# Expert stage of a small language model: first and third products on the two row halves of the array, experts summed on VectorE

## The chip, the cores and the metric

The kernel runs on one core of one Trainium2 chip. The metric is the device time of one execution in microseconds (us). Before the change it is 245.43 us, the median of 3 runs (244.35 to 245.56).

A core has four engines that compute: TensorE (PE in the profile; PEld is its loading of weights), VectorE (DVE), ScalarE (ACT) and GpSimd (POOL). Each works through a program of its own, in order. They wait for each other through semaphores. TensorE writes its results into PSUM, eight banks of 2 KB in each of 128 partitions; the other engines read them there.

## What is computed

The reference is a tower for 8 rows of 256 tokens with 64 channels: a convolution net on embedded tokens, an attention without softmax, and then a transformer block, whose mixture of experts is what the change touches. In float32:

```python
flat = _rmsnorm(x, ln2_w).reshape(-1, Cx)          # 2048 tokens, 64 channels
probs = jax.nn.softmax(flat @ router_w.T, axis=-1)
tp, ti = jax.lax.top_k(probs, TOPK)                # 2 of 8 experts
tp = tp / (jnp.sum(tp, axis=-1, keepdims=True) + 1e-09)
weights = jnp.sum(tp[..., None] * jax.nn.one_hot(ti, NE, dtype=flat.dtype), axis=1)
out = jnp.zeros_like(flat)
for e in range(NE):
    hh = jax.nn.silu(flat @ w1[e].T) * (flat @ w3[e].T)     # 170 hidden channels
    out = out + weights[:, e:e + 1] * (hh @ w2[e].T)
return x + out.reshape(Bx, Tx, Cx)
```

All experts are computed for all tokens; the gate weights, zero for six of eight, choose.

## The kernel before

**Tiling.** The 2048 tokens are 16 tiles of 128, in four groups of four tiles, called pairs in the code (a pair of batch rows, `PAIRS`). The 8 x 170 hidden channels are laid out in `CH` = 11 blocks of up to 128: eight with the first 128 channels of an expert each, three with the remaining 42 channels of up to three experts. A *unit* u (0 to 43) is one pair with one block: 128 hidden channels by 512 tokens, one PSUM bank. Pair n is u // 11, the place in it i = u % 11; `ORDER` (line 18) gives the block.

**Precision.** A float32 value is kept as two float16 numbers, high and low. `fTs` (line 159) holds the transposed normalised input of a tile: the high parts of the 64 channels in partitions 0 to 63, the low parts in 64 to 127. The weights `w1h` and `w3h` (lines 149, 150) lie twice in the partitions, and their index w says high or low. So one matmul over 128 partitions gives (high + low) times the high weight, a second one (high + low) times the low weight.

**One unit** (TensorE's loop is at lines 1909 to 1963) goes through the engines like this:

1. TensorE: two matmuls of 512 columns with `w1h` into a bank of `A_BANK` (0 and 4 in turn), two with `w3h` into a bank of `B_BANK` (3 and 5 in turn).
2. ScalarE, line 814: silu of the first product into `sil`, two buffers in turn.
3. VectorE, line 1330: the third product times `sil`, into `hh`, a ring of six. It is called hh u in the prediction.
4. ScalarE, line 799 (`high_part`): cast of hh u to float16, the high part.
5. GpSimd, line 414 (`low_part`): hh u minus the high part, the low part.
6. TensorE, `down` (line 1844): when the blocks of two experts are there (`FILLED`), their second product for one tile, in three parts (high by high, high by low, low by high), 9 or 12 matmuls of 128 or 64 columns. A bank of `DOWN_BANK` (6 and 1 in turn) holds two experts of four tiles.

ScalarE's loop (line 801) issues silu u and then the cast of u-1. Silu u waits for hh u-2 (line 813). TensorE's first product of u waits for silu u-2, its third product for hh u-2 (lines 1914 to 1921).

**Mixing.** `mix` (line 1254) multiplies a bank of second products with the gate weights into `moe` in SBUF; `mix_add` (line 1261) multiplies the next one in PSUM and adds it to that. So VectorE leaves two partial sums of 512 columns per pair, and TensorE adds them, and the two experts in each, by multiplying with the float32 identity `identf` into bank 2 (`sum_up`, line 1895). `result` (line 1270) adds the residual. The last pair ends in another way (`last_rows_in`, `last_even`, `last_result`, and `last_high` and `last_low` on TensorE), which the change leaves nearly alone.

**Input of a pair.** GpSimd's `third_root` and `third_split` (line 384) make the high and low parts of the normalised rows in `shl`; `f_transposed` on TensorE (line 1720) transposes them into PSUM; `f_rows` on ScalarE (line 741; pairs 0, 2 and 3) or `router_rows` on VectorE (line 1173; pair 1) copies them to `fTs`; `routed` on TensorE (line 1736) gives the router's products, `router_in`, `ranks`, `ranks_end` and `gates` on VectorE the gate weights, with an exponential on ScalarE between (line 746). For pairs 0 and 1 this happens in the attention ahead of the expert stage, beside the batch rows b = 6 and 7 of its loop. For pairs 2 and 3 it is put between units: GpSimd's root after low part 4 and 13, its split after low part 7 and 16 (lines 501 and following), VectorE's rows at u = 7 and 16, the transposes at u = 10 and 20, ScalarE's copy ahead of silu 11 and 21.

The order of all this is written out by hand, in one loop for each engine:

```python
# ScalarE, line 801
for u in range(PAIRS * CH):
    ...
    act.wait_ge(S["a_ps"], u + 1)
    if u >= 2:
        act.wait_ge(S["hh_ready"], u - 1)
    nc.scalar.activation(sil[:, u % 2, :], bank[A_BANK[u % 2]][:, :], ACT.Silu, ...)
    if u:
        high_part(u - 1)
```

## Time and profile before

| | |
|---|---|
| median of 3 runs | 245.43 us (244.35 to 245.56) |
| the profiled execution, its own time | 245.12 us |
| its span in the trace | 243.3 us |
| granted TensorE clock, mean | 0.997 of full speed |
| TensorE matmuls busy | 206.2 us (85% of the span) |
| VectorE busy | 178.8 us (73%) |
| ScalarE busy | 153.6 us (63%) |
| GpSimd busy | 144.1 us (59%) |

The span runs from the first to the last instruction of the trace; 1.8 us of the execution's time lie around it. A matmul's record runs from its start to the end of its result, so two records that follow each other overlap: the step from start to start says how long it holds the array. The same holds for ScalarE and VectorE, whose next instruction can begin some 0.1 us ahead of the end of the last.

### The profile page before, as it was taken

The numbers are of one execution on the slowest core, as the hardware profiler recorded it, in microseconds if no ns is written. First come the engines' busy times: TensorE is split into PE (matmuls) and PEld (weight loads), VectorE is DVE, ScalarE is ACT, GpSimd is POOL, SyncE is SP. The second block draws the span as 40 slices with busy tenths as digits, with TensorE's granted clock in tenths as the row PEclk, the third lists the DMA queues.
The fourth block names the chain that finished last, engine by engine and source line by source line (L and its number), as shares of the span: only waits on it lengthen the run. The fifth ranks groups of instructions, "written<-read, shape, count | busy, mean of one in ns | idle before, by whom it ended". The sixth has DMA issues, their size and how long they took to land.

```text
span 243.3 us, 7308 instructions
## 1 busy us (share of the span) xinstructions
PE 206.2 (85%) x2828; PEld 134.7 (55%) x2836; DVE 178.8 (73%) x417; ACT 153.6 (63%) x277; POOL 144.1 (59%) x196
## 2 busy tenths in 40 slices
PE   7987788888897997976888979988899899888991
PEld 3654446445554755655666757644465465465671
DVE  4224665959878599979975879569868964999586
ACT  2368867277794677876356556577675579576670
POOL 6840000133677657574568896737989784777771
PEclk9999999999999999999999999999999999999998
DMA  2577300000000000000000000000000000010010
GB/s 43 118 164 176 83 5 3 0 3 3 3 1 3 3 3 3 3 3 0 3 3 0 3 0 3 4 0 1 3 3 1 3 23 3 0 24 0 3 24 22
DMA packets 8396, 4.51 MB, mean 19 GB/s; under 512 B 7556, under 2 KB 7852, under 8 KB 8364
## 3 DMA queue, kind: packets, MB, share of 16 engines
q1 hardware_dynamic: 8364, 4.06, 7.3%
q8 instruction: 23, 0.38, 0.6%
q14 instruction: 9, 0.07, 0.1%
HBM read 3.53 MB, written 0.52 MB: 17 GB/s over the span
## 4 chain that ended last, share of the span: by engine, by line
PE 41%; DVE 29%; ACT 12%; issue 10%; POOL 6%; DVEq 0%; POOLq 0%; ACTq 0%
PE bank L1369 39%; DVE shared L1330 3%; DVE nmx L1120 2%; ACT early L671 2%; ACT oTx L662 1%; ACT oT L656 1%; DVE shared L968 1%; DVE L L1297 1%; POOL shared L414 1%; DVE oT L1150 1%; ACT qT L814 1%; DVE early L861 1%; ACT early L565 1%; DVE nmr L1129 1%; DVE s L1167 1%
## 5 line engine op out<-in xcount | busy, mean ns | idle before, releaser
L1369 PE MATMUL bank<-early 64*64 64x256 f32 (+5 forms) x556 | 56.5, 352 | 10.8 <-DVE early L861 2.7
L414 POOL TENSOR_TENSOR shared<-shared 128x512 f16<-128x512 f32 x44 | 51.3, 1166 | 17.1 <-ACT shared L799 14.4
L1369 PEld LDWEIGHTS bank<-early 64*64 64x64 f32 (+3 forms) x556 | 30.7, 126 | 28.4 <-issue 5.2
L1330 DVE SCALAR_TENSOR_TENSOR shared<-bank,qT 128x512 f32<-128x512 f32 x44 | 29.7, 687 | 12.4 <-ACT qT L814 11.5
L799 ACT CAST shared<-shared 128x512 f16<-128x512 f32 x44 | 27.0, 614 | 12.1 <-DVE shared L1330 12.1
L814 ACT ACTIVATE qT<-bank 128x512 f32<-128x512 f32 x44 | 26.3, 597 | 10.5 <-PE bank L1369 10.3
L349 POOL TENSOR_TENSOR stat<-stat,neghalf 128x4 f32<-128x4 f32 x8 | 8.2, 1021 | 37.0 <-DVE stat L946 35.7
L1369 PE MATMUL bank<-onehot,w3h 128*128 128x512 f16 x88 | 26.3, 380 | 3.7 <-DVE shared L1330 3.5
L1369 PE MATMUL bank<-onehot,w1h 128*128 128x512 f16 x88 | 26.2, 379 | 0.3 <-ACT qT L814 0.3
L481 POOL TENSOR_TENSOR oTx<-oT,oTx 128x512 f16<-128x512 f32 x16 | 18.5, 1159 | 13.0 <-ACT oTx L662 12.9
L1369 PE MATMUL bank<-w2xh,shared 128*128 128x128 f16 (+1 forms) x240 | 22.4, 209 | 2.8 <-POOL shared L414 2.4
L1369 PE MATMUL bank<-qT,shared 64*64 64x128 f32 (+1 forms) x320 | 19.0, 326 | 5.5 <-DVE shared L968 2.9
L1369 PE MATMUL bank<-w2h,shared 128*128 128x64 f16 x384 | 22.7, 193 | 0.0
L1369 PEld LDWEIGHTS bank<-w2xh,shared 128*128 128x128 f16 x240 | 15.7, 98 | 10.2 <-POOL shared L414 4.6
L1120 DVE TENSOR_REDUCE nmx<-bank 128x2 f32<-128x512 f32 (+1 forms) x24 | 16.0, 687 | 7.2 <-PE bank L1369 6.9
L732 ACT ACTIVATE qT<-bank 128x512 f32<-128x512 f32 x24 | 14.3, 598 | 8.3 <-PE bank L1369 8.2
L861 DVE TENSOR_TENSOR early<-early 128x512 f32<-128x512 f32 x10 | 6.9, 692 | 17.0 <-ACT early L565 16.5
L1369 PEld LDWEIGHTS bank<-w2h,shared 128*128 128x128 f16 x384 | 18.3, 98 | 0.0
L1369 PEld LDWEIGHTS bank<-qT,shared 64*64 64x64 f32 x320 | 11.1, 132 | 12.8 <-issue 6.8
L656 ACT ACTIVATE oT<-bank 128x512 f32<-128x512 f32 x16 | 9.6, 597 | 12.8 <-PE bank L1369 12.7
L1369 PEld LDWEIGHTS bank<-onehot,w3h 128*128 128x128 f16 x88 | 7.8, 98 | 16.3 <-DVE shared L1330 8.4
L968 DVE TENSOR_TENSOR shared<-bank,trimul 128x512 f32<-128x512 f32 x16 | 11.0, 688 | 6.2 <-PE bank L1369 6.1
(228 smaller groups left out, 460.2 us busy)
## 6 DMA issues: line engine op xcount, KB each, us to landing
early<-in_tcn_w_dram SPq DMA_DIRECT2D x2, 320.0 KB, 4.2
w1s<-in_w1m_dram SPq DMA_DIRECT2D x2, 256.0 KB, 3.6
qT<-in_w3m_dram SPq DMA_DIRECT2D x2, 256.0 KB, 3.8
out_dram<-L SPq DMA_DIRECT2D x8, 64.0 KB, 1.7
qw<-in_attn_q_dram SPq DMA_DIRECT2D x4, 64.0 KB, 2.5
hTs<-in_w2m_dram SPq DMA_DIRECT2D x1, 256.0 KB
cos<-in_cos_t_dram SPq DMA_DIRECT2D x2, 96.0 KB, 2.5
sin<-in_sin_t_dram SPq DMA_DIRECT2D x2, 96.0 KB, 2.4
```

The lines of the kernel that those rows point to most:

```text
L349: nc.gpsimd.tensor_tensor(stat[:, dst, g4], stat[:, src, g4], neghalf[:, 0:4], ALU.pow) \
L414: nc.gpsimd.tensor_tensor(hhx[:, i, 1, :], hh[:, u % RING, :], hhx[:, i, 0, :], ALU.subtract).then_inc(S["lo_ready"], 1)
L481: nc.gpsimd.tensor_tensor(oTx[:, g % 2, 1, :, :], oT[:, g % 2, :, :], oTx[:, g % 2, 0, :, :], ALU.subtract).then_inc(S["o_low"], 1)
L656: nc.scalar.mul(oT[:, g % 2, :, :].rearrange("p a (cc t) -> p cc a t", cc=2), banks[:, 6:8, 0:256].rearrange("p cc (a t) -> p cc a t", a=4 ...
L732: nc.scalar.activation(pT[:, b % 2, u, :], bank[5 + (3 * b + u) % 2][:, :], ACT.Exp).then_inc(S["exp2_ready"], 1)
L799: nc.scalar.copy(hhx[:, i, 0, :], hh[:, u % RING, :]).then_inc(S["hi_ready"], 1)
L814: nc.scalar.activation(sil[:, u % 2, :], bank[A_BANK[u % 2]][:, :], ACT.Silu, scale=1.0 / FFN_SCALE).then_inc(S["sil_ready"], 1)
L861: V_.tensor_tensor(x_, x_, hid2[:, 2 * s:2 * s + 2, :], ALU.add).then_inc(S["x_ready"], 1)
L968: V_.tensor_tensor(om[:, g % 2, :].rearrange("p (x j t) -> p x j t", x=2, t=64), banks[:, 4:6, 0:256].rearrange("p x (j t) -> p x j t", t=64),
L1120: V_.tensor_reduce(nmx[:, g, h0:h0 + nh], bank[4 - (3 * b + u) % 2][:, :].rearrange("p (n s) -> p n s", n=nh), AX, ALU.max, negate=True).t ...
L1330: V_.scalar_tensor_tensor(hh[:, u % RING, :], bank[B_BANK[u % 2]][:, :], HH_SCALE / FFN_SCALE, sil[:, u % 2, :], ALU.mult, ALU.mult).then_ ...
L1369: return nc.tensor.matmul(out_, l_, r_, start=a, stop=z, skip_group_check=skip)
```

## The change

The normalised rows are laid out so that the high parts stand in both halves of the partitions, and in a second block the low parts in both: GpSimd's split writes the two middle parts of the new tile `shf`, a new copy on ScalarE (`f_twice`) writes the outer ones, eight transposes instead of four follow, and `f_rows` and `router_rows` copy 1024 columns instead of 512. The copy for pairs 0 and 1 stands after the exponentials of batch rows 5 and 6, that for pairs 2 and 3 ahead of silu 9 and 19.

A unit has six matmuls of 512 columns over 64 partitions each: the first product on partitions 0 to 63 and the third on 64 to 127, in turn, with the parts high by high, high by low and low by high. The product of the low parts is left out.

From u = 4 the third product has three banks in turn (7, 3, 5), and TensorE waits for hh u-3; `sil` has four buffers, and silu u waits for hh u-4. VectorE adds up the four parts of a pair in one partial sum (`first_mix` to `fourth_mix`) and adds the two experts of it in `result`; `sum_up` is gone. The downs and the mixings stand one to two units later than before. The gates' scratch moves from bank 7 to bank 2. The diff, cut to its core:

```diff
+        shf = shared[:, 9216:10240].bitcast(f16).rearrange("p (x a w c) -> p x a w c", x=2, a=4, w=4)
...
-        fTs = onehot[:, :, :].rearrange("p a b -> p (a b)").bitcast(f16).rearrange("p (g c) -> p g c", c=P)
+        fT2a = onehot[:, :, :].rearrange("p a b -> p (a b)").bitcast(f16).rearrange("p (a x t) -> p a x t", a=2, x=2)
+        fT2b = sTs[:, :, :].rearrange("p g t -> p (g t)").rearrange("p (a x t) -> p a x t", a=2, x=2)
+        fT2 = [fT2a[:, 0], fT2a[:, 1], fT2b[:, 0], fT2b[:, 1]]
...
-        sil = qT[:, :, 3, :]
-        moe = qst[:, :, :, :, :, :].rearrange("p a b c d e -> p (a b c d e)")[:, 0:4 * 2 * NE * C].bitcast(f32) \
-            .rearrange("p (k t e c) -> p k t e c", k=NE // 2, t=4, e=2)
+        sil = [qT[:, 0, 3, :], qT[:, 1, 3, :], qT[:, 0, 0, :], qT[:, 0, 1, :]]
+        moe = qst[:, :, :, :, :, :].rearrange("p a b c d e -> p (a b c d e)")[:, 0:2 * 4 * 2 * C].bitcast(f32) \
...
-        A_BANK, B_BANK, DOWN_BANK, SUM_BANK, LAST_BANK = (0, 4), (3, 5), (6, 1), 2, (0, 7)
-        geP = bank[7][:, 0:256].rearrange("p (a i j) -> p a i j", a=4, j=NE)
-        lP = bank[7][:, 256:288].rearrange("p (a e) -> p a e", a=4)
-        sumP, recP = bank[7][:, 288:292], bank[7][:, 292:296]
+        A_BANK, DOWN_BANK, ROW_BANK, LAST_BANK = (0, 4), (6, 1), 2, (0, 2)
+        geP = bank[2][:, 0:256].rearrange("p (a i j) -> p a i j", a=4, j=NE)
+        lP = bank[2][:, 320:352].rearrange("p (a e) -> p a e", a=4)
+        sumP, recP = bank[2][:, 352:356], bank[2][:, 356:360]
+
+        def third_bank(u):
+
+            return bank[(3, 5)[u % 2] if u < 4 else (7, 3, 5)[(u - 4) % 3]]
...
-                split(shl[:, p % 2, :, :, :], s2[:, p % 2, :, :], "fsplit_ready")
+                split(shf[:, p % 2, :, 1:3, :], s2[:, p % 2, :, :], "fsplit_ready")
...
+            def f_twice(p):
+                act.wait_ge(S["fsplit_ready"], p + 1)
+                nc.scalar.copy(shf[:, p % 2, :, 0:4:3, :], shf[:, p % 2, :, 1:3, :]) \
+                    .then_inc(S["f_twice"], 1)
+
             def f_rows(p, b_):
                 act.wait_ge(S["trf_ps"], p + 1)
-                nc.scalar.copy(fTs[:, 4 * p:4 * p + 4, :].rearrange("p a b -> p (a b)"),
-                               bank[b_][:, 0:256].bitcast(f16)).then_inc(S["fTs_ready"], 1)
+                nc.scalar.copy(fT2[p].rearrange("p x t -> p (x t)"), bank[b_][:, :].bitcast(f16)) \
...
+                if b >= 5:
+                    f_twice(b - 5)
...
+                if u == 9:
+                    f_twice(2)
+                if u == 19:
+                    f_twice(3)
...
-                if u >= 2:
-                    act.wait_ge(S["hh_ready"], u - 1)
-                nc.scalar.activation(sil[:, u % 2, :], bank[A_BANK[u % 2]][:, :], ACT.Silu,
+                if u >= 4:
+                    act.wait_ge(S["hh_ready"], u - 3)
+                nc.scalar.activation(sil[u % 4], bank[A_BANK[u % 2]][:, :], ACT.Silu,
...
+            def weigh(n_, k):
+
+                d_ = downs(DOWN_BANK[k % 2], slice(0, 4))
                 dve.wait_ge(S["w2_ps"], 16 * n_ + 4 * k + 4)
-                link(V_.tensor_tensor(downs(b_, tt), downs(b_, tt), weights_of(n_, k, tt), ALU.mult))
-                dve.wait_ge(S["mix_ready"], 2 * n_ + k // 2 + 1)
-                V_.tensor_tensor(moe[:, k - 1, :, :, :], downs(b_, tt), moe[:, k - 1, :, :, :], ALU.add) \
-                    .then_inc(S["added"], 1)
+                return d_, weights_of(n_, k, slice(0, 4))
+
+            def first_mix(n_):
+                d_, w_ = weigh(n_, 0)
+                V_.tensor_tensor(moe[:, :, :, :], d_, w_, ALU.mult).then_inc(S["mix_ready"], 1)
+
+            def second_mix(n_):
+                d_, w_ = weigh(n_, 1)
+                link(V_.tensor_tensor(d_, d_, w_, ALU.mult))
+                dve.wait_ge(S["mix_ready"], 2 * n_ + 1)
+                V_.tensor_tensor(moe[:, :, :, :], d_, moe[:, :, :, :], ALU.add).then_inc(S["added"], 1)
+
+            def third_mix(n_):
+                d_, w_ = weigh(n_, 2)
+                link(V_.tensor_tensor(d_, d_, w_, ALU.mult))
+                dve.wait_ge(S["added"], n_ + 1)
+                V_.tensor_tensor(moe[:, :, :, :], d_, moe[:, :, :, :], ALU.add).then_inc(S["mix_ready"], 1)
+
+            def fourth_mix(n_):
+                d_, w_ = weigh(n_, 3)
+                link(V_.tensor_tensor(d_, d_, w_, ALU.mult))
+                dve.wait_ge(S["mix_ready"], 2 * n_ + 2)
+                V_.tensor_tensor(d_, d_, moe[:, :, :, :], ALU.add).then_inc(S["odd_mixed"], 1)
 
...
             def result(n_):
 
-                g4 = slice(4 * n_, 4 * n_ + 4)
+                d_, g4 = downs(DOWN_BANK[1], slice(0, 4)), slice(4 * n_, 4 * n_ + 4)
+                dve.wait_ge(S["odd_mixed"], n_ + 1)
                 dve.wait_ge(S["hx_ready"], n_ + 1)
-                dve.wait_ge(S["sum_ps"], 2 * n_ + 2)
-                V_.tensor_tensor(fin[:, g4, :], bank[SUM_BANK][:, 0:256].rearrange("p (t c) -> p t c", c=C),
-                                 hx[:, g4, :], ALU.add).then_inc(S["fin_ready"], 2)
+                link(V_.tensor_tensor(fin[:, g4, :], d_[:, :, 0, :], hx[:, g4, :], ALU.add))
+                V_.tensor_tensor(fin[:, g4, :], d_[:, :, 1, :], fin[:, g4, :], ALU.add).then_inc(S["fin_ready"], 2)
 
...
-                V_.scalar_tensor_tensor(hh[:, u % RING, :], bank[B_BANK[u % 2]][:, :], HH_SCALE / FFN_SCALE,
-                                        sil[:, u % 2, :], ALU.mult, ALU.mult).then_inc(S["hh_ready"], 1)
+                V_.scalar_tensor_tensor(hh[:, u % RING, :], third_bank(u)[:, :], HH_SCALE / FFN_SCALE,
+                                        sil[u % 4], ALU.mult, ALU.mult).then_inc(S["hh_ready"], 1)
                 if u == 2:
                     shares(B - 1)
-                if n_ and i == 1:
-                    mix(n_ - 1, 2, DOWN_BANK[0])
-                if n_ and i == 4:
-                    mix_add(n_ - 1, 3)
-                if n_ and i == 8:
+                if n_ and i == 0:
+                    second_mix(n_ - 1)
+                if n_ and i == 2:
+                    third_mix(n_ - 1)
+                if n_ and i == 5:
+                    fourth_mix(n_ - 1)
+                if n_ and i == 6:
                     result(n_ - 1)
-                if i == 7:
-                    mix(n_, 0, DOWN_BANK[0])
-                if i == 10 and n_ < PAIRS - 1:
-                    mix_add(n_, 1)
+                if i == (8 if n_ < PAIRS - 1 else 7):
+                    first_mix(n_)
...
-                pe.wait_ge(S["fsplit_ready"], p + 1)
+                pe.wait_ge(S["f_twice"], p + 1)
                 if p == 0:
                     pe.wait_ge(S["stk_ready"], TILES)
                 elif p == 1:
                     pe.wait_ge(S["rexp_in"], 1)
-                elif p == 2:
+                else:
                     pe.wait_ge(S["ym_ready"], TILES)
-                else:
-                    pe.wait_ge(S["rexp_in"], 3)
-                    pe.wait_ge(S["fin_ready"], 2)
-                for a in range(4):
-                    r = nc.tensor.transpose(bank[b_][:, 64 * a:64 * a + 64].bitcast(f16),
-                                            shl[:, p % 2, a, :, :].rearrange("p a b -> p (a b)"), ident16[:, :])
+                    pe.wait_ge(S["gate_ready"], p - 1)
+                    pe.wait_ge(S["rexp_in"], p)
+                for x_ in range(2):
+                    for a in range(4):
+                        r = nc.tensor.transpose(bank[b_][:, 256 * x_ + 64 * a:256 * x_ + 64 * a + 64].bitcast(f16),
+                                                shf[:, p % 2, a, 2 * x_:2 * x_ + 2, :].rearrange("p a b -> p (a b)"),
+                                                ident16[:, :])
                 r.then_inc(S["trf_ps"], 1)
 
             def routed(p, b_):
                 pe.wait_ge(S["fTs_ready"], p + 1)
                 c_ = ROUTE_BANK[p][1]
                 for a in range(4):
-                    for w in range(2):
-                        r = mm(bank[b_][:, c_ + NE * a:c_ + NE * a + NE], fTs[:, 4 * p + a, :], rwh[:, w, :], w == 0,
-                               w == 1)
+                    for i, (x_, w) in enumerate(((0, 0), (0, 1), (1, 0), (1, 1))):
+                        r = mm(bank[b_][:, c_ + NE * a:c_ + NE * a + NE], fT2[p][0:64, x_, P * a:P * a + P],
+                               rwh[0:64, w, :], i == 0, i == 3)
...
-                if v >= 2:
-                    pe.wait_ge(S["added" if k % 2 else "mix_ready"], v // 2)
+                if v >= 2 and k != 1:
+                    pe.wait_ge(S["added"] if k == 3 else S["mix_ready"], n_ + 1 if k == 3 else v // 2)
+                if n_ and k == 1:
+                    pe.wait_ge(S["fin_ready"], 2 * n_)
...
-                for w_, banks_, read, done in ((w1h, A_BANK, "sil_ready", "a_ps"), (w3h, B_BANK, "hh_ready", "b_ps")):
-                    if u == 0:
-                        pe.wait_ge(S["wlow_ready"], 2)
-                        pe.wait_ge(S["nmT_ready" if w_ is w1h else "max_ready"], B if w_ is w1h else 3 * B)
-                    if u == 1 and w_ is w3h:
-                        pe.wait_ge(S["exp2_ready"], 3 * B - 1)
-                    if u >= 2:
-                        pe.wait_ge(S[read], u - 1)
-                    for w in range(2):
-                        r = mm(bank[banks_[u % 2]][:, :], w_[:, w, ORDER[i], :], rhs, w == 0, w == 1)
-                    r.then_inc(S[done], 1)
+                if u == 0:
+                    pe.wait_ge(S["wlow_ready"], 2)
+                    pe.wait_ge(S["nmT_ready"], B)
+                if u >= 2:
+                    pe.wait_ge(S["sil_ready"], u - 1)
+                a_, b_ = bank[A_BANK[u % 2]][:, :], third_bank(u)[:, :]
+                mm(a_, w1h[lo_, 0, ORDER[i], :], fT2[n_][lo_, 0, :], True, False)
+                if u == 0:
+                    pe.wait_ge(S["max_ready"], 3 * B)
+                if u == 1:
+                    pe.wait_ge(S["exp2_ready"], 3 * B - 1)
+                if u in (2, 3):
+                    pe.wait_ge(S["hh_ready"], u - 1)
+                if u == 4:
+                    pe.wait_ge(S["ym_ready"], TILES)
+                if u >= 5:
+                    pe.wait_ge(S["hh_ready"], u - 2)
+                mm(b_, w3h[hi_, 0, ORDER[i], :], fT2[n_][hi_, 0, :], True, False)
+                mm(a_, w1h[lo_, 1, ORDER[i], :], fT2[n_][lo_, 0, :], False, False)
+                mm(b_, w3h[hi_, 1, ORDER[i], :], fT2[n_][hi_, 0, :], False, False)
+                mm(a_, w1h[lo_, 0, ORDER[i], :], fT2[n_][lo_, 1, :], False, True).then_inc(S["a_ps"], 1)
+                mm(b_, w3h[hi_, 0, ORDER[i], :], fT2[n_][hi_, 1, :], False, True).then_inc(S["b_ps"], 1)
                 if u == 0:
                     values(B - 1)
                 if u == 1:
                     out_rows(B - 1)
                 if u == 10:
-                    f_transposed(2, SUM_BANK)
+                    f_transposed(2, ROW_BANK)
                 if u == 12:
-                    routed(2, SUM_BANK)
+                    routed(2, ROW_BANK)
                 if u == 20:
-                    f_transposed(3, SUM_BANK)
+                    f_transposed(3, ROW_BANK)
                 if u == 22:
-                    routed(3, SUM_BANK)
-                if n_ and i == 0:
-                    down(n_ - 1, 2, 2)
-                    down(n_ - 1, 2, 3)
-                if n_ and i == 2:
-                    down(n_ - 1, 3, 0)
-                    down(n_ - 1, 3, 1)
-                    sum_up(n_ - 1, 0)
-                if n_ and i == 3:
-                    down(n_ - 1, 3, 2)
-                    down(n_ - 1, 3, 3)
-                if i == 5:
-                    down(n_, 0, 0)
-                    down(n_, 0, 1)
-                if i == 6:
-                    down(n_, 0, 2)
-                    down(n_, 0, 3)
-                    if n_:
-                        sum_up(n_ - 1, 2)
-                if i == 8:
-                    down(n_, 1, 0)
-                    down(n_, 1, 1)
-                if i == 9:
-                    down(n_, 1, 2)
-                    down(n_, 1, 3)
-                if i == 10:
-                    down(n_, 2, 0)
-                    down(n_, 2, 1)
+                    routed(3, ROW_BANK)
+                if n_ and i in (0, 1):
+                    down(n_ - 1, 2, 2 * i)
+                    down(n_ - 1, 2, 2 * i + 1)
+                if n_ and i in (3, 4):
+                    down(n_ - 1, 3, 2 * i - 6)
+                    down(n_ - 1, 3, 2 * i - 5)
+                for k, first in enumerate((6, 9) if n_ < PAIRS - 1 else (5, 8, 10)):
+                    if i in (first, first + 1):
+                        down(n_, k, 2 * (i - first))
+                        down(n_, k, 2 * (i - first) + 1)
```

## Rows read from the trace of the kernel before

**Rows 1.** The page's busy time of each engine, as a share of the span.

```profile
PE 206.2 (85%) x2828; PEld 134.7 (55%) x2836; DVE 178.8 (73%) x417; ACT 153.6 (63%) x277; POOL 144.1 (59%) x196
```

**Rows 2.** Four stretches: length, busy PE, PEld, DVE, ACT, POOL (instructions), granted clock, DMA.

```profile
161.78:179.30 17.52, 15.05 (x168) 8.24 (x167) 14.39 (x31) 12.57 (x24) 14.36 (x15) 1.00 0.01 2
179.30:199.44 20.14, 18.54 (x238) 11.88 (x235) 16.53 (x37) 13.01 (x24) 16.77 (x18) 1.00 0.03 8
199.44:220.75 21.31, 19.33 (x222) 11.57 (x219) 17.12 (x39) 15.50 (x28) 13.94 (x13) 1.00 0.04 8
220.75:235.96 15.21, 14.59 (x192) 10.06 (x192) 11.67 (x25) 10.37 (x19) 11.22 (x11) 1.00 0.04 10
```

**Rows 3.** Groups from 160 us on: count | busy us, mean ns | idle before, its releasers.

```profile
L1330 DVE SCALAR_TENSOR_TENSOR shared<-bank,qT 128x512 f32<-128x512 f32 x44 | 29.7, 687 | 12.4 <-ACT qT L814 11.5 <-POOL shared L414 0.4
...
L1275 DVE TENSOR_TENSOR L<-bank,hx 128x256 f32<-128x256 f32 x3 | 1.2, 415 | 0.0
...
L799 ACT CAST shared<-shared 128x512 f16<-128x512 f32 x44 | 27.0, 614 | 12.1 <-DVE shared L1330 12.1
L814 ACT ACTIVATE qT<-bank 128x512 f32<-128x512 f32 x44 | 26.3, 597 | 10.5 <-PE bank L1369 10.3
...
L1369 PE MATMUL bank<-qst,identf 128*128 128x256 f32 x24 | 6.7, 402 | 0.2 <-DVE lg L1186 0.2
```

**Rows 4.** TensorE's timeline (start us, us, instruction), third row from a window of 20 ns.

```profile
162.07 0.59 PE L1369 MATMUL bank<-onehot,w3h 128*128 128x512 f16 x2
162.60 0.72 PE L1369 MATMUL bank<-wo_sb,yT 64*128 64x130 f32 x8
162.60 0.38 PE L1369 MATMUL bank<-wo_sb,yT 64*128 64x130 f32 x2
162.29 0.38 PE L1369 MATMUL bank<-onehot,w3h 128*128 128x512 f16 x1
163.25 0.39 PE L1369 MATMUL bank<-onehot,w1h 128*128 128x512 f16 x1
...
217.18 0.33 PE L1369 MATMUL bank<-w2xh,shared 128*128 128x128 f16 x3
...
217.86 0.59 PE L1369 MATMUL bank<-onehot,w1h 128*128 128x512 f16 x2
```

**Rows 5.** ScalarE's timeline around silu 24 and its table loads.

```profile
201.29 1.28 ACT L748 ACT_TABLE_LOAD   x1
...
204.24 0.60 ACT L814 ACTIVATE qT<-bank 128x512 f32<-128x512 f32 x1
204.74 0.61 ACT L799 CAST shared<-shared 128x512 f16<-128x512 f32 x1
```

**Rows 6.** GpSimd's timeline: low parts 5 to 7, the split of pair 2, the last head sum.

```profile
172.14 3.71 POOL L414 TENSOR_TENSOR shared<-shared 128x512 f16<-128x512 f32 x3
...
176.39 0.67 POOL L344 TENSOR_TENSOR shl<-s,shl 128x256 f16<-128x256 f32 x1
...
182.50 0.45 POOL L398 TENSOR_TENSOR idx<-oT,xf 128x128 f32<-128x128 f32 x1
```

**Rows 7.** VectorE's timeline: hh 8 and 9, 13 and 14, a linked mixing, hh 22.

```profile
174.75 1.27 DVE L1330 SCALAR_TENSOR_TENSOR shared<-bank,qT 128x512 f32<-128x512 f32 x2
...
184.37 1.28 DVE L1330 SCALAR_TENSOR_TENSOR shared<-bank,qT 128x512 f32<-128x512 f32 x2
...
198.10 0.69 DVE L1265 TENSOR_TENSOR bank<-bank,gate 128x512 f32<-128x512 f32 x1
...
199.44 0.68 DVE L1330 SCALAR_TENSOR_TENSOR shared<-bank,qT 128x512 f32<-128x512 f32 x1
```

**Rows 8.** Ahead of the expert stage: ScalarE's exponentials, TensorE's transposes of pair 1.

```profile
155.85 0.60 ACT L732 ACTIVATE qT<-bank 128x512 f32<-128x512 f32 x1 [0.64 <-PE bank L1369]
159.61 0.23 ACT L748 ACTIVATE lg<-lg 128x32 f32<-128x32 f32 x1 [0.67 <-DVE lg L1186]
155.65 0.39 PE L1732 MATMUL bank<-ident,shl 128*128 128x128 f16 x4
```

41 lines of the change are left out of this document (12 added, 29 removed).

## The prediction

> **What bounds the kernel now.** I read the page's busy shares first: TensorE 85%, VectorE 73%, ScalarE 63%, GpSimd 59% [rows 1]. That average invites "TensorE is the bound, so shorten it", so I cut the expert stage into its four row pairs, each from the start of its first third-product multiplication on VectorE (unit 0, 11, 22, 33; "hh u" below) to the next pair's, the last to the end of hh 43 [rows 2]. TensorE is busy 86%, 92%, 91% and 96% of them, VectorE 82%, 82%, 80% and 77%. The margin is thin: whatever TensorE stops doing, VectorE has only 3 to 4 us to spare in each pair.
>
> The groups say how the engines are tied [rows 3]. VectorE stands idle 12.4 us before its 44 products, 11.5 of them for ScalarE's silu, and ScalarE 10.5 us before the silu, nearly all for TensorE. So there is a ring: TensorE, silu, product, high cast, and back. ScalarE runs silu u, cast u-1, silu u+1 in a fixed order; hence silu u+2 follows cast u, which follows hh u, with two banks or three, with two silu buffers or four. One turn back to back costs 0.69 (product) + 0.03 + 0.50 (cast to silu) + 0.63 (silu to product) = 1.85 us for two units: the silu at 204.24 and the cast at 204.74 give the 0.50 [rows 3, 5]. The change leaves this order as it is.
>
> **TensorE.** Two full-row matmuls of 512 columns last 0.59 us and a single one 0.38, so each takes 0.21 to 0.22 us of the array [rows 4]. A unit has four, 0.865 us. After: six on row halves in three pairs, 0.65 us if the halves overlap. They do where the kernel already uses them: of the 64-row products two begin within 0.01 us (x2 in the window 162.59 to 162.61), and all eight records take 0.72 us [rows 4]. Saved: 44 x 0.216 = 9.5 us. The sums with the identity go too, 24 records of 256 columns at about 0.215: 5.2 us [rows 3]. Added are changes of the array's form. The full-row pair at 162.07 should hand over at 162.50, and the half-row work starts at 162.60: 0.09 us; its last pair starts near 163.04 and takes 0.11, and full rows start at 163.25: 0.10 us [rows 4]. The down products stay on full rows and stand between 29 of the 44 units: 29 x 0.19 = 5.5 us. Net, TensorE loses 9.2 of the 67.5 us that it works in the four stretches. The Trainium skill (TensorEngine Tiling (Array Packing), Key Properties) says that a change of tiling mode drains the engine; the row agrees with 0.09 to 0.10 us.
>
> **VectorE.** Per pair the old mixing is one product, product and add, product, product and add, and one sum of 256 columns; the new one has a further add, and two sums of 256 columns. Back to back a 512-column instruction takes 0.60 to 0.69 us, a linked product and add 1.34 (198.10 to 199.44) [rows 7], the 256-column sum 0.415 [rows 3]. That is +1.0 to 1.1 us in each of three pairs, 3.2 us, on the engine with little to spare. The Trainium skill (TensorEngine Tiling (Array Packing), PSUM Bottleneck) warns that tiling speeds TensorE and not the emptying of PSUM; the rows on ScalarE and VectorE agree, and by that rule alone the 9 us buy nothing.
>
> **ScalarE.** Four doubling copies of 512 columns are new, a cast of that size being 0.61 and 0.50 of it uncovered [rows 3, 5]. The row copy grows from 512 to 1024 columns. No row shows one; from two of 512 (0.50 more) to none: I take +0.4. Two of each fall in this stage.
>
> Now the end, worked in order of time.
>
> **1. Ahead of unit 0: +1.0 us.** Copy 0 fits into ScalarE's idle time near 150. Copy 1 has to stand before the exponential at 155.85, which had 0.64 us of idle before it, and the transposes at 155.65 then wait for it [rows 8]. Before that, eight transposes instead of four (+0.22: four take 0.39, a single one 0.22), 16 router products instead of 8 (+0.2, at most what four transposes take) and their two changes of form (+0.19) delay the exponential at 154.6 by 0.6. So copy 1 runs 155.7 to 156.3; transposes follow, 0.22 longer: values and all behind them on TensorE +0.9. The router products add 0.1 to 0.2. ScalarE waits for just this chain at 159.61 (idle 0.67, for the router's input) and loads the silu table only then [rows 8]. So hh 0 is late by 1.0. Bounds: 0.3 if the idle time takes the copy, 1.3 if nothing is hidden.
>
> **2. Pair 0, to hh 13: +1.6 us.** This is the step that matters. Copy 2 stands ahead of silu 9 and needs GpSimd's split of pair 2. GpSimd runs three low parts back to back from 172.14 and ends the split at 176.39 + 0.67 = 177.06 [rows 6]. Nothing of the change makes it earlier by more than 0.1: low part 4, ahead of them, waits for hh 4, and that for VectorE's ranks. Silu 9 had served hh 9 at 175.35 (the second of the two at 174.75) [rows 7]. After: copy 2 at 177.0, silu 9 at 177.5, hh 9 at 178.1 on the old clock, 2.75 us late. Before, only TensorE waited for this split, and silu and product 9 and 10 went past it. Then, in ScalarE's steps of 0.50: hh 10 at 179.1; the 1024-column copy (0.9) lies ahead of silu 11, so hh 11 at 181.0 instead of 179.30 [rows 2], +1.7. Low part 10 and the head sum follow on GpSimd as before (the sum ended at 182.95 [rows 6]) and end 1.6 late; VectorE waits for them ahead of hh 13, which was at 184.37 [rows 7]. The second mixing, moved to hh 11, fills that wait.
>
> **3. hh 13 to hh 22: +0.4 us.** Before: 199.44 - 184.37 = 15.07 us. After: nine products at 0.60 (5.4), third and fourth mixing (2.7), result (0.8), first mixing (0.6), gates and normalisation (4.15): 13.65 us. The quiet end, hh 17 to 22, is ScalarE's: copy 3, four casts, four silus and the long copy, leaving VectorE idle for about 0.35 + 1.1 + 0.4 = 1.85. Together 15.5.
>
> **4. hh 22 to hh 33: -0.4 us.** The two table loads (1.28 each, the first at 201.29, silu 24 at 204.24) [rows 5] still stand between cast 22 and silu 24. Second mixing and router input fill VectorE until 2.5 after hh 22; hh 24 is at 5.1. From there VectorE has no gap: nine products 5.4, mixings 2.7, result 0.8, first mixing 0.6, two ranks with their ends 5.0, gates 1.3: 20.9 against 21.31.
>
> **5. hh 33 to the end of hh 43: -0.5 us.** Here TensorE was the bound (96%). After: products 6.7, second to fourth mixing 4.0, result, first mixing and last product 2.0, gates 1.3, waits for the ring 0.7: 14.7 against 15.21. The tail behind it has the same instructions: 0.
>
> Sum: 1.0 + 1.6 + 0.4 - 0.4 - 0.5 = **+2.1 us** on the profiled execution's own 245.12, or 247.2. That execution lies 0.3 below the median, so **247.5 us**.
>
> Costed at nothing: the third bank's wait for the last shares (unit 4), since VectorE is still in the first ranks then; the gates' move to bank 2, whose transposes come units apart; the downs one unit later, which keep three units' distance from TensorE to the low parts. Without that cover each would cost a TensorE stall of up to one unit, 0.65 us.
>
> **The rivals.**
> **A, faster: the longer lead wins.** TensorE may run three units ahead on the third product. If that removes half of VectorE's 12.4 us of waiting, then -6.2 + 3.2 + 1.0 = -2.0: 243.4. For it: TensorE's 92 to 96%, and waits that were put down to TensorE. Against: the ring through cast and silu, and GpSimd's late split. It decides if copy 2 stalls silu 9 by under 0.5 us. 20%.
> **B, no difference.** The start costs 0.3 and the quiet units gain what copy 2 loses: 2.1 - 0.7 - 1.2 = +0.2, 245.6. 14%.
> **C, the halves don't overlap.** No row here shows 16-bit row halves with 512 columns, and the 32-bit ones write PSUM at half the rate. Serial, a unit takes 6 x 0.216 = 1.30, 0.43 more than now; 19 us on TensorE less 5.2, plus 5.5: 19 us more work there, 6.7 of it into its idle time (74.2 less 67.5): at least +12, 257. 6%. The Trainium skill (TensorE: Matmul & The Clock Gate, Measured speedup vs the span model) gives 3.07 for four row tiles; an estimate from that, 77% of the ideal, makes a unit 0.84 us, so that TensorE would win nothing.
> **D, the clock.** TensorE would stand still for about 3 us at two places (copy 2, table loads), where now the granted clock is 1.00 throughout [rows 2]. If it falls to 1.2 GHz for a few units, a unit with the downs of two tiles (0.65 + 0.68, from 217.18 to 217.86 [rows 4]) takes 2.7 us instead of 1.33 and TensorE is last: +2 to +4 on top, 250.5. 10%.
> The forecast itself has 50% (own range 246.5 to 249.5).
>
> **Numbers.** 0.5% is 1.2 us, about what a measurement of this kernel can tell from no change. Slower by more: forecast, C and D, 66%. Within: B, 14%. Faster: A, 20%. The range runs from the middle of A, 243.6, to the top of D, 251.0; outside are C, a third of A and the forecast's tail.
>
> **What would show it.** Right: w1h and w3h records in pairs starting within 0.01 us, a unit every 0.65 where nothing waits; about 0.1 us on either side of the downs; in ScalarE's timeline the copy of pair 2 ahead of silu 9, and hh 9 some 16 us behind hh 0 instead of 13.6; VectorE over 90% busy in the last pair; TensorE's busy share of the stage down from 90% to near 70%. Wrong: hh 9 within 14 us of hh 0, or pairs 1 and 2 each a microsecond or more shorter than now; then the ring was not the limit and the time is A's. Records of the halves 0.2 us apart would be C.

## The result, and the profile after

The change made the kernel slower: **251.76 us** median of four executions (250.71 to 252.32) against 245.23 (244.35 to 245.56), a ratio of 1.027 with an interval of 1.024 to 1.029. The profiled execution took 252.28 us, with a span of 250.5. The prediction was 247.5 (243.6 to 251.0): the right sign, too small, and outside its range.

The page after, busy shares, then TensorE, VectorE and the granted clock in 40 slices of 6.3 us:

```profile
PE 205.4 (82%) x2948; PEld 131.2 (52%) x2948; DVE 182.1 (73%) x423; ACT 156.7 (63%) x281; POOL 144.5 (58%) x196
...
PE   8986888777997997877989898878599597879781
...
DVE  4225666969795889798857787479289945999886
...
PEclk9999999999999999988999999999889779999997
```

TensorE's busy time is almost what it was (206.2), although 9.2 us of work were to go. The last row hints at the reason: in the expert stage (from slice 27 on) slices 29 and 30 show 8, and 32 and 33 show 7, so the clock was not whole there; it was 1.00 in all four stretches before [rows 2]. (The two 8s further left are the attention stage, and the 7 at the end lies behind hh 43; the kernel before has a fall there too.) The same four stretches after, cut at hh 0, 11, 22 and 33:

```profile
162.88:182.05 19.17, 13.98 (x177) 7.34 (x174) 12.54 (x29) 13.20 (x25) 14.49 (x15) 0.94 0.01 2
182.05:205.32 23.27, 19.82 (x265) 11.80 (x263) 18.22 (x39) 13.45 (x25) 16.67 (x17) 0.83 0.03 7
205.32:227.23 21.91, 17.62 (x259) 9.90 (x256) 18.00 (x40) 14.80 (x26) 12.97 (x12) 1.00 0.03 8
227.23:243.02 15.79, 13.37 (x217) 8.19 (x214) 13.90 (x29) 11.60 (x21) 12.18 (x12) 1.00 0.04 9
...
179.60:183.00 3.40, 3.40 (x36) 1.96 (x33) 1.75 (x4) 2.92 (x5) 2.62 (x3) 0.50 0.02 5
196.60:203.40 6.80, 5.75 (x57) 3.43 (x58) 4.17 (x9) 4.67 (x9) 3.82 (x4) 0.50 0.10 22
```

Against [rows 2] the stretches are longer by 1.65, 3.13, 0.60 and 0.58 us; with hh 0 later by 1.10 that is the 7.1 us by which hh 43 ended later. The last two rows are two windows with a granted clock of 0.50, the lower of the two levels (1.2 GHz), 10.2 us in all. In them TensorE counts 9.15 us busy for what takes about half as long at the whole clock. By an estimate from that, its busy time in the stage would be 60.2 us at the whole clock and not 64.8, so 7.3 less than the 67.5 of before.

Groups from 160 us on, different shapes apart:

```profile
L1361 DVE SCALAR_TENSOR_TENSOR shared<-bank,qT 128x512 f32<-128x512 f32 x44 | 29.9, 687 | 15.1 <-ACT qT L832 14.6
L813 ACT CAST shared<-shared 128x512 f16<-128x512 f32 x44 | 27.0, 614 | 16.2 <-DVE shared L1361 16.2
L832 ACT ACTIVATE qT<-bank 128x512 f32<-128x512 f32 x44 | 26.2, 595 | 7.6 <-PE bank L1400 6.9 <-DVE shared L1361 0.5
...
L755 ACT COPY sTs<-bank 128x1024 f16<-128x1024 f16 x2 | 2.0, 1022 | 0.0
...
L1763 PE MATMUL bank<-ident,shared 128*128 128x128 f16 x16 | 1.7, 266 | 2.8 <-ACT shared L750 2.8
...
L750 ACT COPY shared<-shared 128x512 f16<-128x512 f16 x2 | 1.2, 616 | 3.3 <-POOL shared L351 3.3
```

Compared with [rows 3]: ScalarE stands idle less before the silu (7.6 us for 10.5), VectorE more before its products (15.1 for 12.4, and of that 14.6 for 11.5 for the silu), and two waits are new: ScalarE's copy for GpSimd's split (3.3) and TensorE's transposes for that copy (2.8). Where that is, in ScalarE's, TensorE's and GpSimd's timelines (start, length, instruction, idle before it):

```profile
173.99 0.62 ACT L813 CAST shared<-shared 128x512 f16<-128x512 f32 x1 [0.39 <-DVE shared L1361]
177.87 0.62 ACT L750 COPY shared<-shared 128x512 f16<-128x512 f16 x1 [3.27 <-POOL shared L351]
178.40 0.59 ACT L832 ACTIVATE qT<-bank 128x512 f32<-128x512 f32 x1
...
206.61 0.60 ACT L832 ACTIVATE qT<-bank 128x512 f32<-128x512 f32 x1 [0.82 <-PE bank L1400]
207.10 0.61 ACT L813 CAST shared<-shared 128x512 f16<-128x512 f32 x1
207.73 1.28 ACT L760 ACT_TABLE_LOAD   x1
...
210.69 0.60 ACT L832 ACTIVATE qT<-bank 128x512 f32<-128x512 f32 x1
```

```profile
174.78 0.25 PE L1400 MATMUL bank<-w2h,shared 128*128 128x64 f16 x3
174.96 0.39 PE L1400 MATMUL bank<-onehot,w1h 64*128 64x512 f16 x1
174.97 0.39 PE L1400 MATMUL bank<-onehot,w3h 64*128 64x512 f16 x1
175.19 0.38 PE L1400 MATMUL bank<-onehot,w1h 64*128 64x512 f16 x1
175.19 0.38 PE L1400 MATMUL bank<-onehot,w3h 64*128 64x512 f16 x1
...
178.54 0.62 PE L1763 MATMUL bank<-ident,shared 128*128 128x128 f16 x8 [2.76 <-ACT shared L750]
...
179.93 0.60 PE L1400 MATMUL bank<-onehot,w1h 64*128 64x512 f16 x1
...
180.33 0.63 PE L1400 MATMUL bank<-onehot,w1h 64*128 64x512 f16 x1
...
194.67 0.39 PE L1400 MATMUL bank<-onehot,w1h 64*128 64x512 f16 x1 [0.31 <-ACT qT L832]
197.66 0.61 PE L1400 MATMUL bank<-onehot,w3h 64*128 64x512 f16 x1 [2.60 <-DVE shared L1361]
```

```profile
177.17 0.67 POOL L351 TENSOR_TENSOR shared<-s,shared 128x256 f16<-128x256 f32 x1
...
194.25 1.15 POOL L421 TENSOR_TENSOR shared<-shared 128x512 f16<-128x512 f32 x1 [0.36 <-POOL shared L421]
```

The halves do run together: w1h and w3h start within 0.01 us, step by 0.22 us (174.96, 175.19), and the change of form costs 0.09 us in front (174.78 + 3 x 0.029 = 174.87, first half at 174.96). But TensorE then stands still for 2.76 us, until the copy behind the split is done. About a microsecond after it starts again the granted clock is at half, and the same step takes 0.40 us (179.93 to 180.33). It stands still again for 2.60 us before 197.66, where the third product of unit 20 waits for VectorE, and the clock is at half from 196.6, within that gap, to 203.4. VectorE's timeline there:

```profile
192.77 0.69 DVE L1361 SCALAR_TENSOR_TENSOR shared<-bank,qT 128x512 f32<-128x512 f32 x1
193.38 0.69 DVE L1297 TENSOR_TENSOR bank<-bank,gate 128x512 f32<-128x512 f32 x1
194.10 0.70 DVE L1299 TENSOR_TENSOR bank<-bank,qst 128x512 f32<-128x512 f32 x1
194.71 0.97 DVE L1185 TENSOR_TENSOR s<-idx,stat 128x256 f32<-128x256 f32 x1
...
196.91 0.69 DVE L1361 SCALAR_TENSOR_TENSOR shared<-bank,qT 128x512 f32<-128x512 f32 x1
```

Between hh 16 and 17 lie 4.13 us, where 2.25 did before: the fourth mixing, the normalisation of pair 3 and the gates of pair 1 in one row. The normalisation (L1185) took 0.97 us instead of 0.41; GpSimd's low part (194.25 to 195.40) ran at the same time, as it had not before, and the normalisation ended 0.28 us after it. The normalisation of pair 2 had such a neighbour in both kernels. It took 1.16 us before (from 173.67) and 0.51 after (from 173.87), and both times it ended 0.28 us after GpSimd's instruction.

### The profile page after: what moved, and what is told of

It reads as the page before. It is cut to its first block, busy times and chain, and to the rows that moved or that the text cites. A ratio compares the mean times of both kernels' runs of the same rounds, so it can differ in the third digit from the quotient of the medians.

```text
span 250.5 us, 7550 instructions
## 1 busy us (share of the span) xinstructions
PE 205.4 (82%) x2948; PEld 131.2 (52%) x2948; DVE 182.1 (73%) x423; ACT 156.7 (63%) x281; POOL 144.5 (58%) x196
## 4 chain that ended last, share of the span: by engine, by line
DVE 31%; PE 28%; ACT 14%; issue 13%; POOL 7%; SPq 4%; DMA 1%; DVEq 0%; POOLq 0%; ACTq 0%
PE bank L1400 25%; DVE shared L1361 4%; POOL shared L421 2%; ACT early L678 2%; DVE nmx L1138 2%; ACT qT L832 2%; ACT oTx L669 1%; ACT shared L813 1%; ACT oT L663 1%; DVE shared L986 1%; DVE L L1328 1%; DMA ew<-in_attn_e_dram 1%; DVE early L879 1%; ACT early L572 1%; DVE oT L1168 1%
## 5 line engine op out<-in xcount | busy, mean ns | idle before, releaser
L1400 PE MATMUL bank<-early 64*64 64x256 f32 (+5 forms) x556 | 57.2, 353 | 9.5 <-DVE early L879 2.9
L1361 DVE SCALAR_TENSOR_TENSOR shared<-bank,qT 128x512 f32<-128x512 f32 x44 | 29.9, 687 | 15.1 <-ACT qT L832 14.6
L1400 PE MATMUL bank<-w2xh,shared 128*128 128x128 f16 (+1 forms) x240 | 23.9, 216 | 4.1 <-POOL shared L421 2.4
L1400 PE MATMUL bank<-w2h,shared 128*128 128x64 f16 x384 | 24.0, 197 | 0.0
L1400 PE MATMUL bank<-onehot,w3h 64*128 64x512 f16 x66 | 19.5, 414 | 4.6 <-DVE shared L1361 3.1
L1400 PEld LDWEIGHTS bank<-w2xh,shared 128*128 128x128 f16 x240 | 14.8, 102 | 16.0 <-POOL shared L421 7.9
L1400 PE MATMUL bank<-onehot,w1h 64*128 64x512 f16 x66 | 19.8, 410 | 0.6 <-ACT qT L832 0.6
L1400 PE MATMUL bank<-sTs,w1h 64*128 64x512 f16 x66 | 18.0, 380 | 2.4 <-ACT qT L832 2.4
L1400 PE MATMUL bank<-sTs,w3h 64*128 64x512 f16 x66 | 17.7, 379 | 2.1 <-DVE shared L1361 2.0
L1400 PEld LDWEIGHTS bank<-w2h,shared 128*128 128x128 f16 x384 | 19.3, 101 | 0.0
```

What stands on the lines that cost most here:

```text
L1361: V_.scalar_tensor_tensor(hh[:, u % RING, :], third_bank(u)[:, :], HH_SCALE / FFN_SCALE, sil[u % 4], ALU.mult, ALU.mult).then_inc(S["hh_re ...
L1400: return nc.tensor.matmul(out_, l_, r_, start=a, stop=z, skip_group_check=skip)
```

## The experiments

Times are medians of four executions unless said, ratios those to the kernel before on the same chip (its medians were 245.06 to 245.50). T is in each the theory that I held, the others its rivals.

**1. The changed kernel without the doubling copies.** The split stays single; each transpose is replaced by two of 64 columns, into either half of the partitions.

```diff
-                pe.wait_ge(S["f_twice"], p + 1)
+                pe.wait_ge(S["fsplit_ready"], p + 1)
...
-                        r = nc.tensor.transpose(bank[b_][:, 256 * x_ + 64 * a:...],
+                        for cols_ in (lo_, hi_):
+                            r = nc.tensor.transpose(bank[b_][cols_, 256 * x_ + 64 * a:...],
```

> The doubling copies are gone: each transpose of 128 columns is done as two of 64 columns, one into each half of the partitions, straight from the split. Theory T (the late copy ahead of silu 9, then TensorE's clock, cost most of the loss): hh 9 comes within 14 us of hh 0 again, TensorE's idle time of 2.8 us ahead of the transposes shrinks to about 1, the first fall of the granted clock is gone; 246.5 to 248.5 us. Rival R (VectorE's extra additions, 3.2 us, are the price and the copies only use time that VectorE would lose anyway): 250 us or more.

250.58 us (249.16 to 251.42), ratio 1.022 [1.017, 1.027]: by the median in the rival's range and outside T's. The trace of the execution of 249.76 us shows something of both: hh 9 is back at 12.6 us behind hh 0 and the fall of the clock there is gone, but the stall has moved to silu 11, behind the row copy that waits for the same split (hh 10 to 11: 4.31 us), and the second fall is still there. TensorE's idle time ahead of the transposes shrank less than T said, and yet the clock stayed whole behind it (first the row, then the stretch from 174.50 to 190.00 with its clock):

```profile
177.17 0.64 PE L1758 MATMUL bank<-ident,shared 128*64 128x128 f16 x16 [2.12 <-POOL shared L351]
174.50:190.00 15.50, 12.37 (x197) 7.45 (x195) 10.55 (x22) 8.61 (x16) 13.33 (x15) 1.00 0.01 3
```

Its executions spread over 2.3 us, so this run alone decides little; run 5 measures the copies better. The rival's reason, VectorE's additions, is not shown by it: the whole change without the row halves costs 2.3 us (run 6).

**2. The changed kernel with two banks for the third product, as before.** The four silu buffers stay, but silu u waits for hh u-2 again, so that only two are in use at a time.

```diff
-            return bank[(3, 5)[u % 2] if u < 4 else (7, 3, 5)[(u - 4) % 3]]
+            return bank[(3, 5)[u % 2]]
...
-                if u >= 4:
-                    act.wait_ge(S["hh_ready"], u - 3)
+                if u >= 2:
+                    act.wait_ge(S["hh_ready"], u - 1)
```

> Only the lead is undone: the third product has two banks again (3 and 5), TensorE's third product and silu u wait for hh u-2. Theory T (the ring of cast and silu sets how far silu can go, whatever the banks): within 1 us of the changed kernel, 251 to 252.8 us. Rival L (three banks and four buffers do save waits of VectorE, and the loss would be larger without them): 254 us or more.

254.13 us (253.68 to 254.38), 1.037 [1.034, 1.039]: the rival's range. The longer lead is worth 2.4 us in the changed kernel, more than I gave it, most of it in the stretch with the half clock: hh 13 to 22 take 19.7 us instead of 18.2.

**3. The kernel before with the row halves and the doubling copies only**, the mixing and the banks as before.

```diff
-                        r = mm(bank[banks_[u % 2]][:, :], w_[:, w, ORDER[i], :], rhs, w == 0, w == 1)
+                mm(a_, w1h[lo_, 0, ORDER[i], :], fT2[n_][lo_, 0, :], True, False)
+                mm(b_, w3h[hi_, 0, ORDER[i], :], fT2[n_][hi_, 0, :], True, False)
...
```

> The kernel before with the row halves alone (and with the doubling copies that they need): the old mixing with the sums on TensorE, two banks, the old places of the downs. Theory T: start +1.1 and the late copy +1.6 to 2.5 remain, VectorE's additions are gone, and TensorE has 5 us more work so that its clock holds: 247 to 249 us. Rival R (the additions are the price): 245 to 246.3 us, no slower than before.

250.25 us (249.84 to 250.64), 1.021 [1.019, 1.024]. The row halves alone, which save TensorE over 9 us of array time before the changes of form, cost 5.2 us. This is more than T's 247 to 249, and the rival's 245 to 246.3 is excluded. The stage has no fall of the clock in this trace, so the clock is no part of it.

**4. The changed kernel, with TensorE kept busy** by products that nobody reads: twelve ahead of the transposes of pair 2, ten at the start of unit 20.

```diff
+                if p == 2:
+                    for _i in range(12):
+                        mm(bank[b_][:, :], w1h[:, 0, 0, :], fT2[1][:, 0, :], True, True)
...
+                for _i in range({20: 10}.get(u, 0)):
+                    mm(a_, w1h[lo_, 0, ORDER[i], :], fT2[n_][lo_, 0, :], True, True)
```

> The changed kernel with matmuls whose result nobody reads in TensorE's two longest waits: 12 of 512 columns ahead of the wait for the copy of pair 2, 10 on row half one at the start of unit 20. Theory T: the granted clock stays at 1.00 through the stage and units 13 to 24 lose what the half clock cost, 2.5 to 4 us: 248 to 249.5 us. Rival K (TensorE is not the bound there, so its clock costs nothing): 251 us or more although the clock is 1.00.

250.13 us (249.68 to 250.63), 1.021 [1.019, 1.024]: 1.6 us less by giving TensorE *more* to do. That lies between T's range and the rival's. In the trace the clock is whole from hh 0 to 219 us (hh 29), and hh 13 to 22 take 16.1 us instead of 18.2. First this stretch in the changed kernel, then here; the clock is the number behind POOL's:

```profile
187.12:205.32 18.20, 14.76 (x184) 8.36 (x181) 13.93 (x31) 10.36 (x20) 12.53 (x13) 0.81 0.04 9
186.71:202.82 16.11, 13.56 (x173) 7.07 (x171) 13.93 (x30) 10.06 (x19) 11.79 (x13) 1.00 0.04 10
```

VectorE is busy for 13.93 us in both. So that stretch of the changed kernel holds 2.1 us of clock. The first fall, at 179.6, cost almost nothing: hh 9 to 13 take 8.10 us with it and 7.99 without. Nor did the fall that this trace still has, 3.4 us from 219.2: hh 22 to 33 take 21.89 us against 21.91.

**5. Row halves in the kernel before, without the doubling copies** (run 3 with the edit of run 1).

> The kernel before with the row halves, the doubling done by transposes of 64 columns into both halves of the partitions, without copies on ScalarE. Theory T: of the 5.2 us of the row halves with copies, the stall at silu 9 (1.6), the late start (0.4 to 1.2) and copy 3 in the quiet units (0.5 to 1) go: 246.5 to 248.5 us. Rival Q (the stall only moves on to the 1024-column copy ahead of silu 11, which waits for the same split): 249 us or more.

248.05 us (247.75 to 248.35), 1.011 [1.009, 1.013]: T's range. The row halves without copies still cost 2.6 us, and the doubling copies 2.2 by the two times (250.25 to 248.05) or 2.6 by the distances from the kernel before on each chip (5.2 and 2.6).

**6. The whole change but the row halves:** three banks, the sums on VectorE, all placements, with full rows and no copies.

```diff
-                mm(a_, w1h[lo_, 0, ORDER[i], :], fT2[n_][lo_, 0, :], True, False)
-                mm(b_, w3h[hi_, 0, ORDER[i], :], fT2[n_][hi_, 0, :], True, False)
...
+                mm(a_, w1h[:, 0, ORDER[i], :], rhs, True, False)
+                mm(a_, w1h[:, 1, ORDER[i], :], rhs, False, True).then_inc(S["a_ps"], 1)
```

> The whole change but the row halves: four full-row matmuls a unit, the old input layout, no doubling copies; the sums on VectorE, three banks, four silu buffers, the later downs stay. Theory T: no stall at silu 9, the clock holds since TensorE has 9.5 us more to do; VectorE's additions and the mixings crowded into the first half of a pair cost 0 to 3 us: 245 to 248 us. Rival R (the additions and their places are the main price): 249 us or more.

247.76 us (246.95 to 248.26), 1.010 [1.007, 1.012]. So the row halves, copies and all, cost 4.0 of the 6.5 us, and the rest of the change 2.3 (247.76 against 245.50, the kernel before on the same chip). The time is in T's range, but T's reading is not borne out: the granted clock falls twice in this trace, from 178.2 and from 195.2, for 3.4 us each. Its timelines show the stall ahead of the first fall; ScalarE first:

```profile
177.88 0.58 ACT L747 COPY onehot<-bank 128x512 f16<-128x512 f16 x1 [1.51 <-PE bank L1748]
179.64 0.60 ACT L818 ACTIVATE qT<-bank 128x512 f32<-128x512 f32 x1 [1.18 <-PE bank L1386]
```

```profile
177.44 0.40 PE L1748 MATMUL bank<-ident,shl 128*128 128x128 f16 x4 [2.01 <-POOL shl L348]
...
178.56 1.04 PE L1386 MATMUL bank<-onehot,w1h 128*128 128x512 f16 x2
```

Two full-row products take 1.04 us here, 0.59 at the whole clock [rows 4]: TensorE had got ahead, to the transposes, and could do nothing of what stands behind them, and silu 11 comes 0.97 us later than in the kernel before. I put this down to the longer lead; the later places of the downs, which change as well, are not told apart from it by any run.

**7. The kernel before with half of TensorE's up-projection left out:** the products with the low parts of w1 and w3, 88 matmuls of 0.216 us, 19 us.

```diff
-                    for w in range(2):
+                    for w in range(1):
```

> The kernel before with one matmul instead of two in each first and third product; the products with the low part of these weights are left out. TensorE has 88 matmuls of 512 columns, 19 us, less to do. Theory T (the ring of silu, product and cast, VectorE's bursts and GpSimd's late split bound the stage; TensorE's time is worth little): 242 to 245 us, at most 3 us gained for 19. Rival P (TensorE bounds the stage, as its 86 to 96% say, and the change lost its gain elsewhere): 239 us or less.

242.29 us (242.14 to 244.02), 0.989 [0.986, 0.993]: T's range. Nineteen microseconds of TensorE are worth 3.2, one sixth. By that measure the 9.2 us that the change was to save on TensorE are worth about 1.5 us, an estimate that takes every microsecond to be worth the same.

**8. The kernel before with the longer lead:** three banks, four silu buffers, and the gates' scratch moved from PSUM to SBUF to free the bank.

```diff
-        geP = bank[7][:, 0:256].rearrange("p (a i j) -> p a i j", a=4, j=NE)
+        geP = gpad[:, 0:256].rearrange("p (a i j) -> p a i j", a=4, j=NE)
...
+            return bank[(3, 5)[u % 2] if u < 4 else (7, 3, 5)[(u - 4) % 3]]
```

> The kernel before with the lead alone: three banks for the third product from unit 4, four silu buffers, and for that the gates' scratch in SBUF instead of bank 7. Theory T (the lead matters only where TensorE is slow): 244 to 246 us. Rival L (undoing the lead cost 2.4 us in the changed kernel, so adding it to the kernel before gains as much): 243 us or less.

255.18 us (254.75 to 255.90), 1.040 [1.038, 1.043], which fits neither theory. The groups of VectorE's gate instructions give a reason:

```profile
L1204 DVE TENSOR_TENSOR gpad<-gpad,lg 128x256 f32<-128x256 f32 x4 | 5.1, 1263 | 0.1
...
L1209 DVE TENSOR_TENSOR gpad<-gpad,sqr 128x256 f32<-128x256 f32 x4 | 2.9, 722 | 0.0
```

The same two instructions took 0.43 and 0.42 us with their scratch in PSUM; in the kernel before they are these:

```profile
L1199 DVE TENSOR_TENSOR bank<-bank,lg 128x256 f32<-128x256 f32 x4 | 1.7, 432 | 0.1
L1204 DVE TENSOR_TENSOR bank<-bank,sqr 128x256 f32<-128x256 f32 x4 | 1.7, 423 | 0.0
```

The mean hides two kinds. L1209 of this run took 0.41 us twice, with GpSimd on no subtraction of 512 columns, and 1.09 and 0.97 beside one; all four of L1204 ran beside one:

```profile
170.86 0.41 DVE L1209 TENSOR_TENSOR gpad<-gpad,sqr 128x256 f32<-128x256 f32 x1
192.53 1.09 DVE L1209 TENSOR_TENSOR gpad<-gpad,sqr 128x256 f32<-128x256 f32 x1
```

Each of the six long ones started behind GpSimd's instruction and ended 0.28 us after it. VectorE's busy time went from 178.8 to 188.4 us, which is nearly the whole loss of 9.7. The run tells of the price of that move and nothing of the lead; what the lead alone does to the kernel before stays open.

**9. Run 1 and run 4 together:** no copies, TensorE kept busy.

> The changed kernel without the doubling copies (each transpose writes both halves of the partitions) and with TensorE kept busy with unread products in two waits: nine ahead of its wait for GpSimd's split of pair 2, ten at the start of unit 20. The copies cost 2.2 us in the kernel before with the row halves, and keeping TensorE busy gave 1.6 us in the changed kernel. Theory T (the two are separate costs and all that the row halves cost): the two together leave what the kernel without the row halves takes, 247.5 to 248.8 us, and the granted clock stays whole from unit 9 to unit 33. Rival (the row halves have a further cost of their own, in the order of the passes or in the transposes): 250 us or more although the clock stays whole.

248.15 us (247.96 to 249.71), 1.015 [1.011, 1.019]. The number is T's; its reading holds only in part. Run 6, to which it compares, has falls of the clock of its own, and here too the clock fell for 3.4 us, from 218.0 (hh 28 to 31), ahead of unit 33. Against run 11, the same kernel with full rows and the clock kept over these waits, 1.7 us are left to the row halves. Their traces show where: hh 0 is 0.46 us later (it has more transposes and router products, but the traces of runs 1 and 9, with the same code up to there, differ by 0.31 and those of runs 6 and 12 by 1.39), and the row copy ahead of silu 21 is longer. First its row here, then in run 11:

```profile
198.89 1.01 ACT L755 COPY sTs<-bank 128x1024 f16<-128x1024 f16 x1
```

```profile
198.48 0.59 ACT L747 COPY onehot<-bank 128x512 f16<-128x512 f16 x1
```

Silu 21 follows at 199.79 and at 198.96; silu 22 then waits 0.48 us for TensorE here, and hh 24 is 1.28 us late, hh 43 1.66.

**10. The square of pair 3 after hh 13 instead of hh 12**, in the kernel before (ten executions) and in the kernel of run 5.

```diff
                 if u == 12:
                     router_in(2)
+                if u == 13:
                     rms_square(3)
```

> The kernel before with one edit: VectorE squares pair 3 after the product of unit 13 instead of after that of unit 12. In the trace of the kernel before the product of unit 13 comes about 1.9 us later than its neighbours' rhythm because the square in front of it waits for GpSimd. Theory T (that wait is a stall of the bounding chain): 243.5 to 245.0 us. Rival N (VectorE or the silus of these units are late anyway, or the normalisation of pair 3 becomes late by as much in its place): 245.0 to 246.0 us.

> The kernel before with the row halves, without doubling copies and with the old mixing (248.05 us by its own run), and with the same edit: the square of pair 3 after the product of unit 13. Theory T (the stall at unit 13 is on the chain in every version): 246.2 to 247.4 us. Rival N (hidden): 247.6 to 248.4 us. Either way, if it stays above the kernel before, the row halves have lost with every repair that was tried.

245.10 us, 0.999 [0.997, 1.001], and 248.28 us, 1.013 [1.011, 1.016]: nothing, both times. The product of unit 13 comes 1.93 us earlier (182.44 for 184.37), and that of unit 14 only 0.16: silu 14 waits for TensorE, which sums the experts of pair 0 just there. Both are the rival's ranges: a wait of the engine that seems last was not on the path.

**11. Run 6 with TensorE kept busy** (six executions), **12. run 6 with pair 2's transposes, row copy and router part one unit later** (ten), and **13. both**, with the unread products at unit 20 alone.

```diff
-                if u == 10:
+                if u == 11:
                     f_transposed(2, ROW_BANK)
...
-                if u == 11:
+                if u == 12:
                     f_rows(2, ROW_BANK)
```

> The whole change but the row halves (247.76 us by its own run), with TensorE kept busy by unread products in two waits: twelve ahead of the transposes of pair 2, ten at the start of unit 20. In the trace without them the granted clock is at half for 3.4 us after each of these waits. Theory T (the clock holds a good part of the 2.4 us by which it is slower than the kernel before): 246.0 to 247.1 us. Rival N (the loss is the wait for GpSimd's split and VectorE's order, and the clock costs nothing here): 247.4 to 248.3 us.

> The whole change but the row halves, with the transposes of pair 2 one unit later on TensorE, the row copy one unit later on ScalarE, and the router's part of pair 2 one unit later on TensorE and VectorE (the square of pair 3 with it). Nothing reads these rows before unit 22. Theory T (unit 11 is late, 4.85 us after unit 10, only because the transposes and the copy stand ahead of it and wait for GpSimd's split): the gap between the products of units 10 and 11 falls under 2.5 us and the time to 245.8 to 247.0 us. Rival N (the wait moves to unit 12 or 13 whole): 247.3 to 248.3 us.

> The same as full_later, with ten unread products at the start of unit 20. Theory T (place and clock add up): 244.5 to 246.2 us, so level with or under the kernel before. Rival N: as full_later within 0.4 us.

246.44 us, 1.003 [1.002, 1.005]; 246.21 us (244.96 to 248.09), 1.003 [1.001, 1.006]; and **244.65 us** (244.41 to 244.72), 0.9960 [0.9945, 0.9975]. All three times are in T's ranges. (Run 12 moves VectorE's router part and its square of pair 3 as well, so its 1.6 us are not the transposes' alone.) In run 13, ScalarE around silu 11:

```profile
176.46 0.60 ACT L818 ACTIVATE qT<-bank 128x512 f32<-128x512 f32 x1 [0.23 <-PE bank L1386]
176.95 0.61 ACT L803 CAST shared<-shared 128x512 f16<-128x512 f32 x1
177.74 0.58 ACT L747 COPY onehot<-bank 128x512 f16<-128x512 f16 x1 [0.17 <-PE bank L1748]
```

Silu 11 starts at 176.46 instead of 179.64, and the copy, now behind it, waits 0.17 us. hh 10 to 11 fall from 4.85 to 1.53 us; part of it comes back at hh 14 (4.16 us behind hh 13), so that hh 16 is 2.1 us earlier than in run 6 and hh 22 2.7. This is the one version with all the work in it that beats both kernels, the kernel before by 0.25% to 0.55%: with VectorE's sums, the longer lead and the ten unread products, and without the row halves.

**14. The same placement in the changed kernel**, its doubling copy ahead of silu 10.

```diff
-                if u == 9:
+                if u == 10:
                     f_twice(2)
...
-                if u == 10:
+                if u == 11:
                     f_transposed(2, ROW_BANK)
```

> The changed kernel, row halves and doubling copies in place, with the same later placement of pair 2's transposes, row copy and router part, and its doubling copy ahead of silu 10 instead of silu 9. Theory T (the copy's wait for the split is what stalls unit 9, and the placement repairs it): 248.5 to 250.5 us against 251.76. Rival N (the copy waits where it stands, and it or the transposes only stall a later unit): 251.0 to 252.5 us.

250.11 us (249.57 to 251.19), 1.020 [1.017, 1.023]: 1.6 us back, in T's range. The wait moves to silu 10 (hh 9 to 10: 3.52 us, where hh 8 to 9 took 4.72) and is shorter, and in the profiled execution, the fastest of the four, the first fall of the clock does not come. The other three had a mean granted clock of 0.972 to 0.974, as low as the changed kernel's, so whether the fall stays away there is not shown.

## Why the prediction was off

The sum was 2.1 us on the profiled execution; measured were 7.2 (252.28 - 245.12). Of the 5 us between them 2.7 lie in step 3, and 1.0 and 1.1 in steps 4 and 5.

**Step 1, +1.0: measured +1.10** at hh 0. The size agrees, but in part by luck: runs 2, 4 and 14 have the same code up to there, and their traces put hh 0 at 163.21, 162.56 and 163.64, so +0.8 to +1.9. A fall of the clock in the attention stage (3.4 us from 111.3) is in the changed kernel's trace; the latest of these traces has none there, so it does not explain the spread.

**Step 2, +1.6 to hh 13: measured +1.65** (24.24 us behind hh 0 instead of 22.59), and by the mechanism: split at 177.84, copy at 177.87, silu 9 at 178.40, hh 9 16.14 us behind hh 0 where "some 16" was forecast. Taking this step in the order of waits, rather than by busy time, is what worked. The fall of the clock at 179.6 lies in it and cost 0.1 us (run 4).

**Step 3, +0.4: measured +3.13, and this is the step that failed.** I put hh 13 to 22 at 15.5 us; they took 18.20. Two terms were missing, put at nothing without a reason. The first is the clock: TensorE waits 2.60 us behind VectorE's row of mixing, normalisation and gates, ahead of unit 20, the clock is at half for 6.8 us with that, and it costs 2.1 us, by run 4. I had listed that row's work, but had added it up as VectorE's time and never asked how long TensorE would stand behind it. The clock was on the list as rival D, at 10%, but not by this path. D named two places with about 3 us of idle time each, copy 2 and the table loads. At copy 2 the idle time (2.76 us) and the fall came, and cost 0.1 us; at the table loads TensorE stood idle for 1.78 us and the clock stayed whole; the fall that cost something came at a third place. D's price, +2 to +4, was at or above what the clock cost: 2.1 us in the stretch, 1.6 by the medians of run 4. The second term is the normalisation of pair 3: 0.97 us instead of the 0.41 of its row, +0.56, because its new place falls beside a low part of GpSimd. Together they are the 2.7 us, and with the clock kept the stretch took 16.1 us, 0.6 above the 15.5.

**Step 4, -0.4: measured +0.60** (21.91 us for 20.9 forecast). The work behind hh 24 was right, 15.91 us against 15.8. Ahead of it hh 24 came 6.0 us behind hh 22 and not 5.1: silu 23 waits 0.82 us for TensorE (206.61), cast 22 and the two table loads start behind it.

**Step 5, -0.5: measured +0.58** (15.79 us for 14.7). VectorE's work was right, 13.9 us against 14.0; the term that failed is the ring's waits, 0.7 us. VectorE stands idle in this stretch for 15.79 - 13.90 = 1.9 us, and is 88% busy, not over 90%. TensorE's work went from 96% to 85% of the stretch, and nothing of it was gained.

**The rivals.** A (the lead wins) did not come, but run 2 shows the lead worth 2.4 us in the changed kernel, and in run 13 lead and sums together come out 0.7 us ahead of the kernel before, once the stall is taken away and the clock kept. B is excluded by the interval. C is excluded by the records' 0.01 us. TensorE's share of the stage was 81% (64.8 of 80.1 us) where near 70% was forecast: part of it is the slow clock, 4.6 us.

**The rule that I had cited.** The Trainium skill (TensorEngine Tiling (Array Packing), PSUM Bottleneck) says that tiling speeds TensorE and not the emptying of PSUM. Runs 3, 5 and 7 agree with what follows from it here: the silu and the product read as much PSUM as before, the row halves gained nothing, and TensorE's time is worth one sixth. That reading PSUM is the limit, rather than the ring through the cast and the waits for GpSimd, no run tells apart. I had cited the rule, and still booked gains in steps 4 and 5.

**The bill,** by differences of medians, which need not add up exactly: of 6.5 us, doubling copies about 2.2 (run 5), row halves besides 1.7 (runs 9 and 11), and the rest of the change 2.3 (run 6), of which 1.3 is the clock (run 11). Runs 6 and 11 to 13 show that this rest is a matter of where pair 2's steps stand and of the clock: with both mended nothing of it is left. Not measured were what the third bank or the sums on VectorE do to the kernel before by themselves, and the row halves without copies in the placement of run 13, so whether they would cost anything there is open.

## What to carry to other kernels

Before cutting the work of the busiest engine, leave half of it out and time that: here 19 us were worth 3.2, and the overhead that the cheaper form needs (a copy ahead of a silu, 2.2 us) was larger than what the saving is worth by that measure (1.5). When an engine gets ahead of its suppliers, ask what is next in its queue: a step that nobody needs for ten units must not stand, with its wait, in front of one that is needed at once. And add up how long TensorE stands idle at each new wait, since the clock at half, which the sum of durations does not show, cost 1.3 to 1.6 us here; then measure, since which idle time brings it down did not follow from its length alone (below).

## What the hardware showed that I had not expected

- With TensorE's idle times of 2.76 and 2.60 us (changed kernel) and 2.01 us (run 6) came stretches of 3.4, 6.8 and 3.4 us with the granted clock at half, the second of them beginning within the idle time; pairs of half-row products then stepped by 0.40 to 0.43 us instead of 0.22. Unread products in those gaps kept it whole there and were worth 1.6 us (run 4), 1.3 (run 11) and 1.6 (runs 12 and 13).
- The length of the idle time did not decide it. After 2.12 us (run 1, from 175.1) and 2.17 us (run 2, from 176.7) the clock stayed whole, and after 2.19 us (run 2, from 195.7) it was at half for 6.8. In the traces of runs 4, 9 and 13 it fell for 3.4 us between 215 and 223 us, with no idle time over 1.8 us near. The changed kernel and run 11, whose idle times there are those of runs 4 and 13 (1.78 and 1.71 us, 1.24 and 1.49), have no such fall.
- VectorE's `tensor_tensor` of 256 columns with both tensor operands in SBUF took up to three times as long when it started behind a subtraction of 512 columns on GpSimd: 0.97 us for 0.41 (L1185), 1.16 for 0.42 (the kernel before, L1167), and 1.26 for 0.43 in run 8, where only the scratch had moved from PSUM to SBUF. It ended 0.28 us after GpSimd's instruction each time, so its length was set by how much of that one was left. With an operand in PSUM it took 0.43 us beside the same subtraction.
- Row halves of 64 x 512 in 16 bit overlap completely, and a transpose of 64 columns can write either half of the partitions, which makes the doubling copies unnecessary.
